# Turning x and a third of g on VectorE instead of TensorE in an adapter plus mixture-of-experts kernel

## What is computed

```
out  = x @ W_base.T + b_base + 2 * lora(x, cond_8)          # E*R = 128 low-rank rows
gate = softmax(out @ gate_w.T); best two of 8, weights to a sum of 2.5
g    = silu(out @ w_gate[e]) * (out @ w_up[e])              # F = 352 columns
y    = sum over the two of weight * (g @ w_down[e])
out2 = x + y + (silu(out @ sw_gate) * (out @ sw_up)) @ sw_down   # 704 columns
```

## Time and profile before

| engine | busy us | share of the span | instructions |
|---|---|---|---|
| TensorE, matmuls | 486.3 | 99% | 3071 |
| TensorE, weight loads | 450.1 | 92% | 3072 |
| VectorE | 351.2 | 72% | 786 |
| ScalarE | 262.0 | 53% | 526 |
| GpSimd | 220.3 | 45% | 231 |

### The profile page before, as it was taken

How to read it: one execution, slowest core, us unless ns; L and a number is a source line. 1 busy time by engine, 2 the same in 40 slices (tenths; PEclk the granted TensorE clock), 3 DMA queues, 4 the chain that set the end, 5 groups by cost and what they waited for, 6 DMA issues and landing times.

```text
span 490.9 us, 9830 instructions
## 1 busy us (share of the span) xinstructions
PE 486.3 (99%) x3071; PEld 450.1 (92%) x3072; DVE 351.2 (72%) x786; ACT 262.0 (53%) x526; POOL 220.3 (45%) x231
## 2 busy tenths in 40 slices
PE   9999999999999999999999999999999999999997
PEld 8999988888888899999999999999999999888886
DVE  3557866889887547677777767776777776489896
ACT  3577876566563445576555555555554553445322
POOL 2052237655551354655776556556556652211100
PEclk9999999999999999999999999999999999999999
DMA  7498569472222235544444444444444451699932
GB/s 194 152 299 240 174 181 322 152 221 87 44 86 44 87 85 132 127 120 118 125 112 117 128 118 118 118 124 115 114 118 128 120 118 56 174 384 321 385 129 85
DMA packets 104953, 74.53 MB, mean 152 GB/s; under 512 B 61963, under 2 KB 99861, under 8 KB 104917
## 3 DMA queue, kind: packets, MB, share of 16 engines
q1 hardware_dynamic: 97712, 55.20, 38.7%
q0 software_dynamic: 6816, 18.62, 13.1%
q10 hardware_dynamic: 388, 0.27, 0.2%
HBM read 40.25 MB, written 20.32 MB: 123 GB/s over the span
## 4 chain that ended last, share of the span: by engine, by line
PE 99%; DVE 0%; DVEq 0%; issue 0%
PE bank L286 24%; PE bank L287 24%; PE bank L288 24%; PE bank L834 10%; PE bank L836 5%; PE bank L806 5%; PE bank L598 1%; PE bank L610 1%; PE bank L606 1%; PE bank L607 1%; PE bank L629 1%; PE bank L744 1%; PE bank L743 1%; PE bank L762 0%; PE bank L643 0%; PE bank L661 0%
## 5 line engine op out<-in xcount | busy, mean ns | idle before, releaser
L571 POOL DMA_INDIRECT y_rows<-y_sb,dst_i x71 | 70.0, 985 | 74.3 <-DVE y_sb L1411 73.7
L286 PE MATMUL bank<-w_all,rt_h 128*128 x284 | 97.6, 344 | 0.0
L288 PE MATMUL bank<-w_all,rt_l 128*128 x284 | 91.7, 323 | 0.0
L287 PE MATMUL bank<-w_all,rt_h 128*128 x284 | 91.5, 322 | 0.0
L565 POOL DMA_INDIRECT rows<-x_halves,tok_i x71 | 68.6, 967 | 31.1 <-issue 20.9
L834 PE MATMUL bank<-w_all,gt_h 128*128 (+1 forms) x213 | 77.7, 396 | 0.0
L1004 ACT CAST gt_h<-bank 128x512 fp32r<-128x512 f32 (+1 forms) x47 | 27.5, 586 | 85.3 <-DVE bank L1314 76.8
L286 PE MATMUL bank<-xs_h,sg_h 128*128 128x512 f32 x176 | 70.4, 400 | 0.0
L287 PE MATMUL bank<-xs_l,sg_h 128*128 128x512 f32 x176 | 68.9, 391 | 0.0
L288 PE MATMUL bank<-xs_h,sg_l 128*128 128x512 f32 x176 | 68.7, 390 | 0.0
L1398 DVE TENSOR_TENSOR g<-bank,act 128x352 f32<-128x352 f32 x71 | 37.3, 525 | 39.6 <-ACT act L1031 37.7
(11 more groups left out here) (193 smaller groups left out, 1117.9 us busy)
## 6 DMA issues: line engine op xcount, KB each, us to landing
pick<-y_rows SPq DMA_DIRECT2D x16, 512.0 KB, 7.8
x_halves<-x_half SPq DMA_DIRECT2D x8, 512.0 KB, 3.2
xin<-in_x_dram SPq DMA_DIRECT2D x7, 512.0 KB, 5.1
w_own<-in_L_ffn_w_gate_dram SPq DMA_DIRECT2D x8, 352.0 KB, 4.3
w_own<-in_L_ffn_w_up_dram SPq DMA_DIRECT2D x8, 352.0 KB, 4.6
y_sb<-in_x_dram SPq DMA_DIRECT2D x5, 512.0 KB, 3.5
base_rows<-y_sb SPq DMA_DIRECT2D x5, 512.0 KB, 2.8
acc<-base_rows SPq DMA_DIRECT2D x5, 512.0 KB, 7.7
```

The lines of the kernel that those rows point to most:

```text
L286: pe.matmul(o, lh, rh, start=start, stop=False, skip_group_check=skip)
L287: pe.matmul(o, lh, rl, start=False, stop=False, skip_group_check=skip)
L288: return pe.matmul(o, ll, rh, start=False, stop=stop, skip_group_check=skip)
L571: pool.indirect_dma_start(y_dram, bass.IndirectOffsetOnAxis(ap=dst_i[:, i:i + 1], axis=0), y_sb[:, i % 4, :], None).then_inc(s_sc[i % 4], 16)
```

## The change

The transposes of x for groups 1 to 7, and of the third chunk of g for blocks 0 to 66 (NSQ = 67; the last DIRECT = 4 keep the old way), leave TensorE. VectorE's transpose turns squares of 32x32.

For x, `load_x(i)` lays the rows so that each quarter of the partitions holds a quarter of the channels (four DMAs of 256-byte pieces instead of one of 1 KB pieces), and VectorE's `turn_x(i, k)` turns all squares of the group with one instruction for each of two interleaved sets of channels. The buffer `xt_w` lies where `xt_l` lies. ScalarE's copy now reads it from SBUF, and the subtraction `x_low(i)` goes from VectorE to GpSimd. Group 1 is loaded behind `b_raw` and `bias`.

For g, VectorE's `squares_of_g(i)` turns 128x96 within squares, SP stores the 48 KB to DRAM and loads them back into order (`store_squares`, `load_squares`), ScalarE's `rest_high` and GpSimd's `rest_low` split them, and TensorE multiplies them LAG = 3 blocks later (`e_down_rest`). Results of four blocks are open at once in NYE = 4 banks, `e_y` runs four iterations behind instead of two, and GpSimd gathers seven blocks ahead of its iteration instead of five.

Around it, the splits of routed expert 0 and of the last shared weights move to later places, and some routing steps with them.

```diff
@@ SyncE
+                if i == 2:
+                    sp.wait_ge(s_tx, K)
+                elif i >= 3:
+                    sp.wait_ge(s_xturn, K * (i - 2))
+                from_rows = x_rows[i * GT:(i + 1) * GT, :].rearrange("(a r) (q m) -> q r a m", r=32, m=QC)
+                for q in range(4):
+                    sp.dma_start(squares(i)[q * 32:(q + 1) * 32], from_rows[q]).then_inc(s_xin[i % 2], 16)
...
+            def store_squares(b):
+                sp.wait_ge(s_sq, b + 1)
+                sp.dma_start(g_dram[b].rearrange("(p f) -> p f", p=P), sq[b % 2][:, 0:REST]).then_inc(s_sqst, 16)
+
+            def load_squares(b):
+                sp.wait_ge(s_sqst, 16 * (b + 1))
+                sp.wait_ge(s_D, n_done(b - 2) if b >= 2 else UE)
+                sp.dma_start(gw[b % 2][0:REST, :].rearrange("p (q r) -> p q r", q=4),
+                             g_dram[b].rearrange("(q p r) -> p q r", q=4, r=32)).then_inc(s_gw[b % 2], 16)
...
             for i in range(4):
                 turn_rows(i)
+            store_squares(0)
             store_base(NPG - 1)
+            load_squares(0)
+            store_squares(1)
             for i in range(4, NBLK):
                 turn_rows(i)
+                if i - 3 < NSQ:
+                    load_squares(i - 3)
+                if i - 2 < NSQ:
+                    store_squares(i - 2)
@@ GpSimd
+            def x_low(i):
+                for k in range(K):
+                    pool.wait_ge(s_txh, K * i + k + 1)
+                    pool.tensor_tensor(xt_l[i % 2][:, k, :], xt_w[i % 2][:, k, :], xt_h[i % 2][:, k, :].bitcast(F32), ALU.subtract
+                                       ).then_inc(s_txl, 1)
+            for i in range(1, NG):
+                x_low(i)
+                if 2 <= i < 6:
+                    shared_low(i - 2)
...
-            for i in range(5):
+            def rest_low(b):
+                pool.wait_ge(s_gwh, b + 1)
+                pool.tensor_tensor(gt_l[b % 2][0:REST, REST_COLS], gw[b % 2][0:REST, :],
+                                   gt_h[b % 2][0:REST, REST_COLS].bitcast(F32), ALU.subtract).then_inc(s_gwl, 1)
+
+            for i in range(7):
                 gather(i)
+            for b in range(LAG - 1):
+                rest_low(b)
             for i in range(NBLK):
-                if i + 5 < NBLK:
-                    pool.wait_ge(s_act, UE + i + 2)
-                    gather(i + 5)
+                if i + 7 < NBLK:
+                    pool.wait_ge(s_act, UE + i + 4)
+                    gather(i + 7)
                 if 14 <= i < 14 + 4 * K:
                     split_low_part(NPG, *divmod(i - 14, 4))
                 scatter(i)
+                if i + LAG - 1 < NSQ:
+                    rest_low(i + LAG - 1)
@@ TensorE
             def e_turn_g(i):
                 pe.wait_ge(s_g, i + (UE + 1))
-                for c in range(FC):
+                for c in range(FULL if squared(i) else FC):
...
+            def e_down_rest(i, at, e):
+                pe.wait_ge(s_gwl, i + 1)
+                down_chunk(i, at % 2, YE[at % NYE], FC - 1, FC * P, e).then_inc(s_D, 1)
+
+            def e_step(i, at, es, following):
                 e_turn_g(i - 1)
-                e_next = e_gate_up(i, par, e, following)
-                e_down(i - 1, 1 - par, e_prev)
+                e_next = e_gate_up(i, at % 2, es[-1], following)
+                if not known(i, LAG) and squared(i - LAG):
+                    e_down_rest(i - LAG, at - LAG, es[0])
+                e_down(i - 1, at - 1, es[-2])
@@ ScalarE
             for i in range(NG):
+                if 1 <= i < NG - 1:
+                    x_high(i + 1, 0)
                 hw_high(i)
                 if i == 0:
                     second_factor()
+                    x_high(1, 0)
+                if i + 1 < NG:
+                    x_high(i + 1, 1)
...
+            def rest_high(b):
+                sc.wait_ge(s_gw[b % 2], 16 * (b // 2 + 1))
+                sc.copy(gt_h[b % 2][0:REST, REST_COLS], gw[b % 2][0:REST, :]).then_inc(s_gwh, 1)
...
                 e_high(i - 1)
                 if i + 1 < NBLK:
                     r_high(i + 1)
+                if 0 <= i - LAG < NSQ:
+                    rest_high(i - LAG)
@@ VectorE
+            def turn_x(i, k):
+                if k == 0:
+                    v.wait_ge(s_xin[i % 2], 64 * ((i + 1) // 2) + (16 if i % 2 == 0 else 0))
+                    if i >= 2:
+                        v.wait_ge(s_p, TG * (i - 2) + 1)
+                v.transpose(xt_w[i % 2][:, k, :].rearrange("p (a r) -> p a r", r=32),
+                            squares(i).rearrange("p a (j k) -> p a j k", k=K)[:, :, :, k]).then_inc(s_xturn, 1)
...
             for i in range(NG):
+                if 1 <= i < NG - 1:
+                    turn_x(i + 1, 0)
                 lora_weigh(i)
+                if 1 <= i < NG - 1:
+                    turn_x(i + 1, 1)
                 hw_low(i)
...
+            def squares_of_g(i):
+                v.wait_ge(s_g, UE + i + 1)
+                if i >= 2:
+                    v.wait_ge(s_sqst, 16 * (i - 1))
+                v.transpose(sq[i % 2][:, 0:REST].rearrange("p (q r) -> p q r", r=32),
+                            g[:, MAIN_F:F].rearrange("p (j q) -> p q j", j=32)).then_inc(s_sq, 1)
...
             for i in range(1, NBLK):
                 if i + 1 < NBLK:
                     r_word_low(i + 1)
-                if i >= 2:
-                    e_y(i - 2)
+                if i > LAG:
+                    e_y(next(ys))
...
                 e_low(i - 1)
                 if i + 1 < NBLK:
                     r_low(i + 1)
                 e_mul(i)
+                if i < NSQ:
+                    squares_of_g(i)
```

More of the change, by code:

```diff
@@ L1 @@
 from contextlib import ExitStack
+from itertools import chain
 import concourse.bass as bass
@@ L56, in adaln_moe @@
     TURN = 12
+    DIRECT = 4
+    NSQ = NBLK - DIRECT
+    MAIN_F = FULL * P
+    LAG = 3
+    NYE = 4
     WARM = 7
@@ L238, in adaln_moe @@
         s_y = sem("s_y")
+        s_sq, s_sqst, s_gwh, s_gwl = sem("s_sq"), sem("s_sqst"), sem("s_gwh"), sem("s_gwl")
+        s_gw = [sem(f"s_gw{i}") for i in range(2)]
         s_sc = [sem(f"s_sc{i}") for i in range(4)]
@@ L263, in known, with n_done @@
             return isinstance(i, int) and i < below
+        done_order = []
+        for n in range(NBLK):
+            if 0 <= n - LAG + 1 < NSQ:
+                done_order.append(n - LAG + 1)
+            if n >= NSQ:
+                done_order.append(n)
+        assert sorted(done_order) == list(range(NBLK))
+        def n_done(i):
+            return UE + done_order.index(i) + 1
+        REST_COLS = slice(FC * P, (FC + 1) * P)
         def unit(j, c):
@@ L527, in split_low_part @@
                     ins.then_inc(s_xsl, 1)
[L529 removed]
+            def x_low(i):
[7 more added lines that the diff above has]
+                    shared_low(i - 2)
+            split_low(0)
+            for i in range(4, N_SPART):
                 shared_low(i)
[L531 to L532 removed]
             pool.wait_ge(s_x1, NT)
@@ L840, in e_step, with down_chunk @@
-            def e_step(i, par, e_prev, e, following):
-                e_turn_g(i - 1)
-                e_next = e_gate_up(i, par, e, following)
-                e_down(i - 1, 1 - par, e_prev)
-                return e_next
-            kept = [pe.alloc_register(f"expert{n}") for n in range(2)]
-            def keep(*es):
+            def down_chunk(i, par, to, c, at, e):
+                n = P if c < FULL else REST
+                cols = slice(at, at + P)
+                both = w_all[0:n, :, bass.ds(e, 1), GU + c * D:GU + (c + 1) * D].rearrange("p h e d -> p h (e d)")
+                high = w_all[0:n, 0, bass.ds(e, 1), GU + c * D:GU + (c + 1) * D].rearrange("p e d -> p (e d)")
+                pe.matmul(to[:, 0:2 * D].rearrange("p (h d) -> p h d", h=2), gt_h[par][0:n, cols], both,
+                          start=(c == 0), stop=False, skip_group_check=True)
+                return pe.matmul(to[:, 0:D], gt_l[par][0:n, cols], high, start=False, stop=(c == FC - 1),
+                                 skip_group_check=True)
@@ new lines, in e_down @@
+            def e_down(i, at, e):
+                pe.wait_ge(s_gl, i + (UE + 1))
+                if known(i, NYE):
+                    if i >= 2:
+                        pe.wait_ge(s_fin, 2 * NPG)
+                else:
+                    pe.wait_ge(s_y, i - (NYE - 1))
+                for c in range(FULL if squared(i) else FC):
+                    mm = down_chunk(i, at % 2, YE[at % NYE], c, c * P, e)
+                if not squared(i):
+                    mm.then_inc(s_D, 1)
+            def e_down_rest(i, at, e):
+                pe.wait_ge(s_gwl, i + 1)
+                down_chunk(i, at % 2, YE[at % NYE], FC - 1, FC * P, e).then_inc(s_D, 1)
@@ L850, in keep @@
+            def e_step(i, at, es, following):
+                e_turn_g(i - 1)
+                e_next = e_gate_up(i, at % 2, es[-1], following)
```

(9 more changed lines are left out.)

217 lines of the change are left out of this document (110 added, 107 removed).

## The result

The changed kernel takes 550.82 us (median of 4 runs, 547.43 to 555.74) where the kernel before takes 497.15 us beside it: a ratio of 1.104, 95% interval 1.099 to 1.109. That is 10.4% slower; 556 us were predicted. The ratio leaves out the one slow execution of 555.74 us, so it is not the quotient of the two medians. The profiled execution took 552.33 us with a span of 550.6 us.

The account below looks back on a forecast made before the run. TensorE, 99% of the span, bounds the kernel before; after the change a ring over two blocks does. 64.4 - 0.8 - 5.4 = +58 us gives span 549, time 556 us; the ring's range is 536 to 583.

Parts of the forecast that it names:

- The ring: Block stage: words m-2, `rest_high`, `rest_low`, gather m, DMA transpose, words m; 8.62 us per two blocks, +64.4 us, chance 0.85.
- DMA transpose to words: Ring term from issue of a block's DMA transpose to ScalarE's copied words: 3.5 us, ends 3.3 and 3.64.
- the 64 pitches: Block stage, words of blocks 7 to 70: 32 ring turns, 275.8 us where 211.4 us stood.
- The clock: Rival, block stage: TensorE idle a quarter of each block drops to 1.2 GHz, over 700 us in all; chance 0.02.
- Projection: Projection stage: 56 transposes of x removed, 6.1 us, less a 0.7 us wait; gain 5.4 us, between 0 and 6.1.
- wait of 0.7 us foreseen in the first group: Projection: x 1 loads behind two `b_raw` issues and the bias issue, so TensorE waits about 0.7 us.
- From span to time: Whole kernel: median of runs lies 7.1 us above the profiled span, so span 549 gives 556 us.
- The port: Block stage: by the shared-port rule `r_low` and `rest_low` exclude one another, ring up to 0.42 us longer, 569 us.
- The gather is not held: Rival, block stage: the gather stays at its early place and everything is covered, -12, 486 us; chance 0.09.
- SyncE's queue sets the pace: Rival, block stage: DMA transpose m waits behind `store_squares(m-3)`, 3.41 us per block, +2, 500 us; chance 0.04.

Follow-up runs that it names:

- gather_ahead: Changed kernel with GpSimd gathering eight blocks ahead instead of seven, nothing else changed: 512.54 us, 1.025 of before.
- rest_high_first: Changed kernel with `rest_high` first in ScalarE's iteration, ahead of `r_word_high`, instead of third: 506.03 us, 1.011 of before.
- queue_only: Changed kernel with `load_squares` and `store_squares` one block later on SyncE's queue, behind the DMA transpose; gathers still seven ahead: 544.94 us, 1.106 of before.
- x_gathers_five_ahead: x_only with gathers five blocks ahead instead of seven, `e_y` still four behind: 775.78 us, 1.574 of before.
- behind_gather: Changed kernel with two idle GpSimd subtractions right behind the gather in 58 iterations: 543.44 us, 1.083 of before.
- no_squares_dma: Changed kernel with gathers eight ahead and the squares' store and load removed, compute instructions kept (third chunk wrong): 501.07 us, 0.996 of before.
- x_only: Changed kernel without the part on g (NSQ = 0), x still turned by VectorE: 492.74 us, 0.983 of before; measured again 488.59 us, 0.992.

## Why the prediction was right

**The ring: right, and shown.** Its pieces, the place (`rest_low` ahead of the gather) and the waits came as written: the gather starts 0.15 to 0.19 us behind the end of `rest_low` in 59 of 65 blocks, L1129 waits for the DMA transpose, and TensorE waits ahead of `e_down_rest` for GpSimd. Opening it in either of two places gives most of the loss back.

**Its length: right in the sum, by two errors that cancelled.** Predicted 8.62 us per turn, measured 8.60. The prediction's path from the word copy to the gather, 1.24 + 0.05 + 0.47 + 0.30 = 2.06 us, is 0.92 + 1.11 = 2.03 in the median, though inside it the set-up of the indirect DMA is 0.17 and not 0.30, and `rest_low` 0.53 and not 0.47. Gather to DMA transpose is 3.09 for 3.06. The mis-sized term is DMA transpose to words: 2.38 us in the median and 2.81 in the mean, not 3.5. With it the same sum gives 7.5 us, 32 x 7.5 = 240 us for the 64 pitches, and 556 - 36 = 520 us in all, below the stated range. What filled the gap stood nowhere in the working: `e_high` waits for TensorE, which makes ScalarE's piece 0.5 us longer in the mean. The hit of 275.3 on 275.8 is partly luck.

**The clock: under-rated.** It had 0.02 and was treated as all or nothing. It fell 13 times between 209 and 452 us, each time behind a piece of 1.7 to 2.6 us in which TensorE was idle, and came back each time, 0.92 to 0.93 in the mean of the block stage. So TensorE stood waiting for `rest_low` only 40.7 us in all, 0.6 us per block, where 1.1 us per block were predicted; part of the rest went into slower matmuls. It did not become the bound.

**Projection: 4.1 us, not 5.4.** The mis-sized term is SyncE's. Four issues of x were to take about 2 us of its queue; from 20 us on they take 2.6 to 4.3 (timeline of SyncE's queue in the changed kernel, projection):

```profile
27.82 4.30 SPq L367 DMA_DIRECT2D xin<-in_x_dram  x4
...
35.42 3.50 SPq L367 DMA_DIRECT2D xin<-in_x_dram  x4
```

The DMA engines are busy 0.92 of this stretch where they were 0.71. VectorE's turn waited 5.4 us in all for x, 1.73 and 1.99 us of it at 35.16 and 42.06 us; behind these two TensorE stood idle for `hw_low`, 0.59 us at 37.87 and 0.86 us at 44.76, and the groups (by the start of `lora_in`) are 6.64 and 6.90 us apart. Where x was in time they are 5.77 and 5.78, better than the 5.85 of the prediction. In gather_ahead, whose projection is the same code, these issues took 2.6 to 3.0 us, TensorE did not wait for `hw_low`, and the blocks began at 175.9 us, 5.6 us sooner than before. The wait of 0.7 us foreseen in the first group was 0.28 us, for `xt_l`. The turn itself was 0.70 us where 0.68 was taken, and GpSimd's subtraction 1.29 for 1.31.

**From span to time: wrong by 5 us.** The prediction added 7.1 us to the span, the distance from the profiled span to the median of other runs. Every profiled run of this study lies only 1.7 to 2.1 us above its own span, so most of the 7.1 was scatter between executions. The predicted span was 549 us and 550.6 came out.

**The port.** `rest_low` of the changed kernel took 0.55 us in the mean of 67 (in the profile's group above), and the lone GpSimd subtraction of the same width before took 0.465; in rest_high_first, where `rest_low` meets `r_low` once in 67, it takes 0.47 in the mean. In the changed kernel nearly every `rest_low` meets `r_low`, and the more they overlap the longer the second one takes: 0.52 us where it starts 0.21 us behind `r_low`, 0.58 at 0.15, and 0.69 at 0.03:

```profile
314.68 0.42 DVE L1494 TENSOR_TENSOR rt_l<-rt_w,rt_h 128x256 fp32r<-128x256 f32 x1
314.71 0.69 POOL L662 TENSOR_TENSOR gt_l<-gw,gt_h 96x128 fp32r<-96x128 f32 x1 [1.53 <-ACT gt_h L1144]
```

Twice `rest_low` came first, by 0.05 us (220.3 and 381.4 us): then it kept its 0.45 us, and `r_low` took 0.68 and 0.69 instead of 0.42. So the meeting costs the ring 0.08 us in the mean, 32 x 0.08 = 3 us, and not 0.42 a turn. The Trainium skill, SBUF — State Buffer, "Who interferes with whom", calls the shared port pair an exclusive lock and says that the order of issue decides who is blocked. The traces agree that the second one is held up, but by 0.69 - 0.47 = 0.22 us in the row above, about half of the 0.39 us for which the two overlap, and not by all of it.

**The rivals.** "The gather is not held" is refuted in the changed kernel; where the experiments made it so, the saving it promised did not come (512, not 486), because it counted the squares' DMAs and work as hidden (and its sum takes the 0.7 us off twice, since 5.4 is 6.1 - 0.7). "SyncE's queue sets the pace" was right that the queue is held, but through `load_squares`, not `store_squares`, and queue_only shows that it costs nothing here.

## What to carry to other kernels

Before work is put into an in-order queue, write down what the instruction behind it feeds, and follow that back to the queue: if it closes, the loop's length over the blocks it spans is the pace, however idle each engine is. Moving one instruction past another on one of the queues opens it (shown here on GpSimd's and on ScalarE's). Looking further ahead helps only by the number of blocks that the loop then spans: with seven blocks this ring spans two and costs 54 us, with eight it spans three and costs little. A ring over two blocks is two rings; reckon with their bunching, and read the terms' medians and means apart.

## What the runs showed of the chip

- **TensorE's clock falls behind idle pieces of some us.** Granted clock of TensorE in three short stretches of x_gathers_five_ahead, before and behind its idle time from 402.8 to 406.7 us (columns as in the earlier trace rows):

```profile
399.60:402.70 3.10, 3.10 (x21) 2.82 (x19) 0.16 (x1) 0.00 (x0) 1.11 (x2) 1.00 0.24 85
406.70:411.10 4.40, 4.36 (x18) 4.21 (x19) 0.57 (x2) 0.00 (x0) 1.52 (x2) 0.62 0.16 60
411.10:411.80 0.70, 0.70 (x5) 0.49 (x3) 0.00 (x0) 0.00 (x0) 0.00 (x0) 0.97 0.67 155
```

  After 3.9 us of idling the clock is at a mean of 0.62 for 4.4 us of work, the 1.2 GHz level for most of them, and then back at the 2.4 GHz level. The changed kernel shows the same in its pairs: behind the 1.94 us wait that ends at 307.42 the stretch from 308 to 310 us has 0.64 (though not every such wait does it: six idle pieces of 1.6 to 1.8 us had no fall behind them):

```profile
308.00:310.00 2.00, 2.00 (x11) 1.91 (x10) 1.10 (x4) 0.75 (x3) 1.40 (x2) 0.64 0.43 86
...
312.00:314.00 2.00, 2.00 (x14) 1.88 (x13) 1.30 (x4) 0.73 (x2) 0.99 (x1) 1.00 0.46 134
```

  behind_gather, just as busy (86% from 180 to 420 us), but idle in shorter pieces (5 of over 1.5 us in its block stage, where the changed kernel has 19), has 0.99 in that stretch:

```profile
180.00:420.00 240.00, 207.15 (x1195) 183.12 (x1196) 149.71 (x360) 99.22 (x303) 193.12 (x291) 0.99 0.50 122
```

  The Trainium skill, TensorE: Matmul & The Clock Gate, "What's actually happening", has just two levels, 1.2 GHz for an idle and 2.4 GHz for a busy engine; 1.00 and about half of it are what these stretches are mixed from.
- **VectorE's fp32 turn** of 32x32 squares takes 306 ns for 128x96 and 699 ns for 128x512, where a subtraction of that size takes 682.
- **An indirect DMA** starts 0.15 to 0.19 us behind `rest_low` on GpSimd (59 of 65 blocks of the changed kernel), and 0.30 behind another indirect DMA.
- **DMA transpose to word copy** comes in two lengths. In the changed kernel it took 3.45 us in the median of the 20 blocks for which a gather was issued between 0.6 us before and 0.45 us after the DMA transpose, and 2.36 us in the median of the 42 others; 18 of those 20 are the first of a pair, so the pairs make their own turns longer. Before, all 29 of those for which ScalarE waited had such a gather: 3.5 us in the median, hence the prediction's term. In x_gathers_five_ahead none had: 2.34 to 2.44 us in all 61. It is a coincidence in time and not shown as the cause, and not the whole of it: in gather_ahead, with no gather so near, it took 3.05 us in the median of 38.
- **Left open:** what starts the bunching and keeps it up (it went away where work was added on either side of the gather, and queue_only excludes SyncE's held queue; that the clock, or the slower DMA transposes, feed it was not tried by itself), and how the last 0.004 to 0.013 between no_squares_dma and x_only divide over the three engines.
